# Query and key projections in thirds instead of halves, the keys' three pieces in one period, and the keys' split one period later

## The chip, the cores and the metric

One core of a Trainium2 chip runs the kernel. The metric is the device time of one launch in microseconds (us), lower is better. A core has five engines, each with its own program in its own order: PE (TensorE, matrix products), DVE (VectorE), ACT (ScalarE), POOL (GpSimd) and SP (SyncE, which only issues DMA transfers here). They wait for one another through semaphores.

## The reference

16 sequences of 512 tokens with 128 features go through one transformer layer in float32: attention with 16 heads of 8 features, then a mixture of 8 experts of which each token uses two, each followed by a residual sum and a layer norm.

```python
def attn(x, Wq, bq, Wk, bk, Wv, bv, Wo, bo):          # x: 16 x 512 x 128, 16 heads, dk = 8
    Q, K, V = heads(x @ Wq.T + bq), heads(x @ Wk.T + bk), heads(x @ Wv.T + bv)
    scores = jnp.einsum('bhqd,bhkd->bhqk', Q, K) / jnp.sqrt(jnp.float32(dk))
    probs = jax.nn.softmax(scores, axis=-1)
    intervened = probs.at[:, :, :, 0].set(0.0)
    intervened = intervened / jnp.clip(intervened.sum(axis=-1, keepdims=True), 1e-09, None)
    combined = probs + 0.5 * (intervened - probs)
    ...
    return attn_out @ Wo.T + bo
x = layernorm(x + attn(x, ...))
x = layernorm(x + moe(x, ...))       # 8 experts of 512, two for each token, silu(x w1) * (x w3) w2
```

## The kernel before

The kernel has an attention stage up to about 760 us, in which routing to the experts goes on beside it, an expert stage of 78 tiles of rows up to about 1131 us, and a final sum and layer norm.

**Units and periods.** A sequence's 16 heads are worked on in four groups of four; a group of a sequence is a unit, 64 in all. The attention stage is a pipeline of periods, one for each unit p = 4b + g (PERIODS, from -2 on). Here the periods g = 0, 1, 2, 3 of a sequence b are called its first, second, third and fourth. A period has eight steps k. In period p the unit p + 2 has its row maxima found (a bfloat16 product of queries and keys into the four banks of `mx_ps`, 128 queries at a time, in steps 0, 2, 4 and 6 on PE, L632, each followed by one DVE reduction over 128x2048 numbers, L1016); the unit p has its scores computed one bank at a time (L643) and turned into exponentials by ACT (L837); and the unit p - 1 has these multiplied with the values (L655), in the odd steps. The next `maxima` on PE waits for DVE's reduction, since there is one `mx_ps`.

**The ring.** Scores and all small products share three banks of PSUM, `ring_ps`, as a ring. Every product has a number (`ring_at`), which goes up in program order. PE may write number n when ACT is done with number n - 3; ACT empties them in the same order.

**The pieces behind.** The small products of other sequences are put behind the second score of a step, by the table `BEHIND`: (period in the sequence, step) gives a name and a distance in sequences. `q0`, `q1`, `k0` and `k1` are the projections of queries and keys, each of half of the 512 tokens (L673); q0, q1 and k0 of sequence b + 3 stand in the fourth period of b, and k1 of b + 2 in the first of b. `v0`, `v1` are the values of b + 1, `wo0`, `wo1` the output projection of b - 1, `px` a count for the routing. `BEFORE` lists those of sequence 0 ahead of the first period, `ONCE` those of the first periods -2 and -1. ACT adds the bias on the way out to `full` (L855). In the first period ACT also has `normed_rows` of b - 2 (L901) in every odd step.

**The split.** Queries and keys are split into three bfloat16 parts on POOL: `split_lead` (L1404: a cast, L1412, and a subtraction, L1414) and `split_rest` (L1416: L1421, L1423). SP stores the parts to memory (`store_parts`), from where they are loaded again by head for later units. For sequence 0 DVE does the split (`lead`, L988).

**Order on POOL.** It is written out by hand, for each of the four periods (L1585 to L1657). `beside_reduction(p, w)` makes POOL wait until PE has filled `mx_ps` for the w-th reduction of the period. In the first period the queries' lead stands beside reduction 0, their rest beside 2, and the keys' lead beside 3, followed by a scatter of routed rows. In the second period come `finish_sent` of b - 2 and a scatter beside reduction 0, `split_negmax` of the next unit (L1399, L1401), `product_of_sums` of b - 1 (L1454) and a scatter beside 1, `normalise_second` (L1459) beside 2. The keys' rest stands in the third period beside 2.

**Order on DVE.** Beside the reductions: in the second period `second_sums` (L1032) after reduction 0 and `reciprocals` (L1037) after reduction 1. The latter has its own wait, for POOL's product:

```python
            def reciprocals(b):
                dve.wait_ge(s_norm, NORM * b + 2)
                V.reciprocal(recips[:, 0, :], recips[:, 0, :]).then_inc(s_norm, 1)
```

## Time and profile before

| | us |
|---|---|
| three runs | 1175.75, 1178.43, 1179.16 |
| median | 1178.43 |
| the profiled execution, time | 1177.16 |
| the profiled execution, span from the first to the last instruction | 1175.0 |

Busy over the span: PE 1116.9 us (95%), DVE 927.2 (79%), ACT 824.8 (70%), POOL 663.2 (56%). The granted clock of TensorE is full (2.4 GHz) nearly all the time (0.997 on the mean).

In the profile, times are us from the start of the span unless marked ns; L673 is line 673 of the kernel. A row of the timeline has the start, the duration, the engine, the line, the operation, what it writes and reads, how often in a row (x4 is four instructions that are shown as one), and in brackets how long the engine was idle before and who ended that. Instructions of an engine overlap in part, so that one may start before the one ahead of it has ended. A float32 product appears as two records with half of the work each.

### The profile page before, as it was taken

The page shows a single profiled execution, that of the slowest core. Times are in us where ns is not written, and L with a number is a line of the kernel's source. Part 1 is how long each engine was busy: PE and PEld are TensorE (multiplying, and loading weights), DVE is VectorE, ACT ScalarE, POOL GpSimd, SP SyncE. Part 2 cuts the span into 40 slices and gives each one's busy share as a digit, 9 for nine tenths or more (in the row PEclk, how much of TensorE's full clock was granted, in tenths as well). Part 3 has the DMA queues.
Part 4 walks back from the last instruction along what each step waited for, and adds up shares of the span by engine and source line. Part 5 has one row for each costly group of instructions (what it writes and reads, how often), then busy time and mean ns, then how long its engine had stood idle before and what let it go on. Part 6 is the DMA issues. An engine that isn't in the chain of part 4 may idle for free. (4 is left out here: it accounts for less than half of the span.)

```text
span 1175.0 us, 23587 instructions
## 1 busy us (share of the span) xinstructions
PE 1116.9 (95%) x7236; PEld 575.7 (49%) x7240; DVE 927.2 (79%) x1421; ACT 824.8 (70%) x1668; POOL 663.2 (56%) x1003
## 2 busy tenths in 40 slices
PE   9999999999999999999999998999999999999986
PEld 6422232232222222222322222279999999999962
DVE  6888999999999999999999999855545554444435
ACT  2588888988889889888889888853544434345627
POOL 4424556666676676676676654666545433334336
PEclk9999999999999999999999999999999999999998
DMA  4453334444434343443443345353434333332247
GB/s 145 148 159 112 106 119 124 132 126 127 126 119 138 117 134 117 131 130 109 135 129 125 123 144 159 92 120 84 89 77 103 87 76 80 78 71 58 58 152 301
DMA packets 175051, 139.79 MB, mean 119 GB/s; under 512 B 89539, under 2 KB 151623, under 8 KB 174928
## 3 DMA queue, kind: packets, MB, share of 16 engines
q1 hardware_dynamic: 165672, 119.95, 36.3%
q0 software_dynamic: 8688, 18.14, 4.6%
q8 instruction: 60, 0.98, 0.4%
q14 instruction: 63, 0.52, 0.1%
q10 hardware_dynamic: 568, 0.20, 0.1%
HBM read 95.96 MB, written 42.19 MB: 118 GB/s over the span
## 5 line engine op out<-in xcount | busy, mean ns | idle before, releaser
L837 ACT ACTIVATE probs_sb<-ring_ps 128x512 f32<-128x512 f32 x1024 | 558.4, 598 | 96.9 <-PE ring_ps L643 81.1
L1016 DVE TENSOR_REDUCE rowmax_sb<-mx_ps 128x4 f32<-128x2048 f32 x256 | 586.0, 2289 | 26.3 <-PE mx_ps L632 20.7
L643 PE MATMUL ring_ps<-region_sb 74*128 74x512 bf16 x1024 | 311.4, 384 | 2.1 <-ACT probs_sb L837 2.0
L655 PE MATMUL acc_ps<-probs_sb,values_sb 128*32 128x512 f32 x2048 | 272.3, 604 | 0.0
L1690 POOL DMA_INDIRECT y_d<-probs_sb,values_sb x135 | 133.0, 985 | 190.0 <-DVE probs_sb L1329 166.0
L643 PEld LDWEIGHTS ring_ps<-region_sb 74*128 74x128 bf16 x1024 | 79.2, 97 | 312.8 <-ACT probs_sb L837 272.4
L912 ACT ACTIVATE xT_sb<-region_sb 128x512 f32 x78 | 49.2, 630 | 183.1 <-PE mx_ps L762 181.7
L1329 DVE SCALAR_TENSOR_TENSOR probs_sb<-ring_ps,values_sb 128x128 f32<-128x128 f32 x135 | 42.1, 347 | 143.2 <-issue 120.9
L1546 POOL DMA_INDIRECT rows_d<-sent_sb,pos_sb x128 | 130.1, 1016 | 41.2 <-issue 19.2
L632 PE MATMUL mx_ps<-k_maxima_sb,q_maxima_sb 32*128 32x512 bf16 x1024 | 101.0, 384 | 40.4 <-DVE rowmax_sb L1016 39.9
L783 PE MATMUL ring_ps<-region_sb,probs_sb 128*128 x1080 | 133.5, 275 | 1.6 <-DVE probs_sb L1339 1.6
L783 PEld LDWEIGHTS ring_ps<-region_sb,probs_sb 128*128 128x128 f32 x1080 | 131.0, 192 | 5.0 <-issue 2.2
L752 PE MATMUL mx_ps<-k_parts_sb,xT_sb 128*128 128x256 f32 (+1 forms) x624 | 130.5, 352 | 1.0 <-DVE k_parts_sb L1311 1.0
L1339 DVE TENSOR_TENSOR probs_sb<-mx_ps,probs_sb 128x512 f32<-128x512 f32 (+1 forms) x156 | 95.2, 619 | 25.9 <-PE mx_ps L762 18.6
L752 PEld LDWEIGHTS mx_ps<-k_parts_sb,xT_sb 128*128 128x128 f32 x624 | 106.8, 190 | 13.9 <-DVE k_parts_sb L1311 2.2
L655 PEld LDWEIGHTS acc_ps<-probs_sb,values_sb 128*32 128x32 f32 x2048 | 40.5, 108 | 97.9 <-issue 97.5
L632 PEld LDWEIGHTS mx_ps<-k_maxima_sb,q_maxima_sb 32*128 32x128 bf16 x1024 | 25.7, 90 | 111.7 <-DVE rowmax_sb L1016 102.8
L958 ACT ACTIVATE probs_sb<-mx_ps 128x1024 f32<-128x1024 f32 (+1 forms) x78 | 70.4, 903 | 4.5 <-PE mx_ps L752 4.4
L762 PE MATMUL mx_ps<-k_parts_sb,full_q_sb 128*128 128x256 f32 (+1 forms) x312 | 65.5, 353 | 0.0
L762 PE MATMUL mx_ps<-k_parts_sb,full_k_sb 128*128 128x256 f32 (+1 forms) x312 | 64.6, 350 | 0.0
L762 PEld LDWEIGHTS mx_ps<-k_parts_sb,full_q_sb 128*128 128x128 f32 x312 | 51.6, 191 | 5.3 <-issue 0.8
L1399 POOL CAST negmax_parts_sb<-negmax_sb 16x128 bf16<-16x128 f32 x64 | 17.9, 279 | 62.9 <-PE mx_ps L632 62.7
(193 smaller groups left out, 1174.6 us busy)
## 6 DMA issues: line engine op xcount, KB each, us to landing
region_sb<-q_parts_d SPq DMA_DIRECT2D x64, 288.0 KB
region_sb<-k_parts_d SPq DMA_DIRECT2D x64, 288.0 KB
k_parts_d<-k_parts_sb SPq DMA_DIRECT2D x46, 256.0 KB, 2.5
k_maxima_sb<-k_parts_d SPq DMA_DIRECT2D x128, 64.0 KB
probs_sb<-y_d SPq DMA_DIRECT2D x32, 256.0 KB, 6.9
q_maxima_sb<-q_parts_d SPq DMA_DIRECT2D x126, 64.0 KB
values_sb<-rows_d SPq DMA_DIRECT2D x57, 132.0 KB, 2.3
q_parts_d<-q_parts_sb SPq DMA_DIRECT2D x15, 384.0 KB
```

The lines of the kernel that those rows point to most:

```text
L632: last = nc.tensor.matmul(mx_ps[:, j, :], q[rows, P * c:P * (c + 1)], k[rows, :], start=True, stop=True)
L643: nc.tensor.matmul(bank, KS[b % 2][0:KR + MR, h, P * c:P * (c + 1)], QS[b % 2][0:KR + MR, h, :], start=True, stop=True).then_inc(s_ring_re ...
L655: last = nc.tensor.matmul(acc_ps[VW * j:VW * (j + 1), 0, :], VE[b % 2][:, c, HG * g + j, :], PT[u % 2][:, j, c, :], start=(c == 0), stop=( ...
L752: last = nc.tensor.matmul(up_ps[:, c, 0:n], W1T[t % 2][:, P * c:P * (c + 1)], XGT[t % 2][:, 0:n], start=True, stop=True)
L762: last = nc.tensor.matmul(lin_ps[:, c, 0:n], W3T[t % 2][:, P * c:P * (c + 1)], XGT[t % 2][:, 0:n], start=True, stop=True)
L783: last = nc.tensor.matmul(y_ps[:, at:at + D], HH[t % 2][:, c, P * w:P * (w + 1)], W2[:, bass.ds(expert + c * D, D)], start=(c == 0), stop= ...
L837: nc.scalar.activation(PT[u % 2][:, i // QC, i % QC, :], ring_bank("st", u, i), ACT.Exp, scale=SCALE).then_inc(s_ring_done, 1)
L958: nc.scalar.activation(SG[t % 2][:, :, 0:n], up_ps[:, :, 0:n], ACT.Silu).then_inc(s_silu, 1)
L1016: V.tensor_reduce(rowmax[u % 2][:, :].rearrange("p (j c) -> p j c", c=QC)[:, :, c], mx_ps[:, :, :], axis=AXX, op=ALU.max, negate=True).the ...
L1339: V.tensor_tensor(HH[t % 2][:, part, 0:n], lin_ps[:, part, 0:n], SG[t % 2][:, part, 0:n], ALU.mult)\
L1546: G.indirect_dma_start(rows_d, bass.IndirectOffsetOnAxis(ap=pos[b % 2][:, s, c:c + 1], axis=0), XE[b % 2][:, c, s, :], None).then_inc(s_sc ...
L1690: G.indirect_dma_start(y_d, bass.IndirectOffsetOnAxis(ap=XG[t % RING][:, w, D:D + 1].bitcast(i32), axis=0), YO[t % YRING][:, w, :], None, ...
```

## The change

- `half` becomes `third`: tokens 0 to 176, 176 to 344 and 344 to 512. Queries and keys are projected in three pieces each, q0, q1, q2, k0, k1, k2; a piece is written to its own columns of its bank.
- `BEHIND`: q0, q1, q2 of b + 3 in the fourth period, in the steps where q0, q1 and k0 stood. k0, k1, k2 of b + 2 in the first period, steps 3, 5 and 7, where only k1 stood, in step 3.
- `BEFORE` and `ONCE` have the new pieces; the keys of sequence 1 now stand in the first three steps of period -1.
- Who waited for q1 or k1 waits for q2 or k2.
- On POOL the keys' `split_lead` moves from the end of the first period (beside reduction 3) to the second period, right after the wait for its reduction 0, ahead of `finish_sent`.

```diff
-        BEHIND = {(0, 3): ("k1", 2), (1, 3): ("v0", 1), (1, 5): ("v1", 1), (1, 7): ("px", -2),
-                  (2, 5): ("wo0", -1), (2, 7): ("wo1", -1), (3, 3): ("q0", 3), (3, 5): ("q1", 3), (3, 7): ("k0", 3)}
-
-        BEFORE = (("q0", 0), ("q1", 0), ("k0", 0), ("k1", 0))
+        BEHIND = {(0, 3): ("k0", 2), (0, 5): ("k1", 2), (0, 7): ("k2", 2), (1, 3): ("v0", 1), (1, 5): ("v1", 1), (1, 7): ("px", -2),
+                  (2, 5): ("wo0", -1), (2, 7): ("wo1", -1), (3, 3): ("q0", 3), (3, 5): ("q1", 3), (3, 7): ("q2", 3)}
+
+        BEFORE = (("q0", 0), ("q1", 0), ("q2", 0), ("k0", 0), ("k1", 0), ("k2", 0))
         ONCE = {(-2, 1): ("gc", 0), (-2, 2): ("gw", 0), (-2, 3): ("v0", 0), (-2, 4): ("v1", 0), (-2, 5): ("q0", 1),
-                (-2, 6): ("q1", 1), (-2, 7): ("k0", 1), (-1, 0): ("k1", 1)}
+                (-2, 6): ("q1", 1), (-2, 7): ("q2", 1), (-1, 0): ("k0", 1), (-1, 1): ("k1", 1), (-1, 2): ("k2", 1)}
...
-        def half(name):
-            return slice(L // 2 * int(name[1]), L // 2 * (int(name[1]) + 1))
+        def third(name):
+            edges = (0, 176, 344, L)
+            return slice(edges[int(name[1])], edges[int(name[1]) + 1])
...
-                    last = nc.tensor.matmul(bank[:, 0:L // 2], (wq_sb if name[0] == "q" else wk_sb)[:, :],
-                                            xT_sb[b % 2][:, half(name)], start=True, stop=True)
+                    last = nc.tensor.matmul(bank[:, third(name)], (wq_sb if name[0] == "q" else wk_sb)[:, :],
+                                            xT_sb[b % 2][:, third(name)], start=True, stop=True)
...
-                    done = nc.scalar.activation(full[which][:, half(name)], bank[:, 0:L // 2], ACT.Identity,
+                    done = nc.scalar.activation(full[which][:, third(name)], bank[:, third(name)], ACT.Identity,
...
-                pool.wait_ge(s_ring_done, ring_at[("q1", "k1")[which], b] + 1)
+                pool.wait_ge(s_ring_done, ring_at[("q2", "k2")[which], b] + 1)
...
                     beside_reduction(p, 3)
-                    if is_seq(b + 2):
-                        split_lead(b + 2, 1)
                     scatter_chunk(b - 3, 1)
                 elif g == 1:
                     beside_reduction(p, 0)
+                    if is_seq(b + 2):
+                        split_lead(b + 2, 1)
                     if is_seq(b - 2):
                         finish_sent(b - 2)
                     scatter_chunk(b - 3, 2)
```

## Rows read from the trace of the kernel before

**Rows 1.** Windows, first period: length, busy PE, PEld, DVE, ACT, POOL, clock, DMA.
```profile
404.51:415.80 11.29, 10.34 (x68) 2.65 (x67) 11.09 (x15) 10.63 (x25) 7.88 (x10) 1.00 0.41 129
```

**Rows 2.** Timeline of DVE in the second period of b = 8.
```profile
415.80 2.29 DVE L1016 TENSOR_REDUCE rowmax_sb<-mx_ps 128x4 f32<-128x2048 f32 x1
418.01 0.27 DVE L1032 SCALAR_TENSOR_TENSOR recips_sb<-TN_sb 128x64 f32<-128x64 f32 x1
...
418.60 2.29 DVE L1016 TENSOR_REDUCE rowmax_sb<-mx_ps 128x4 f32<-128x2048 f32 x1 [0.23 <-PE mx_ps L632]
420.81 0.54 DVE L1037 RECIPROCAL recips_sb<-recips_sb 128x64 f32<-128x64 f32 x1
421.47 2.29 DVE L1016 TENSOR_REDUCE rowmax_sb<-mx_ps 128x4 f32<-128x2048 f32 x1
...
424.33 2.29 DVE L1016 TENSOR_REDUCE rowmax_sb<-mx_ps 128x4 f32<-128x2048 f32 x1
...
427.20 2.29 DVE L1016 TENSOR_REDUCE rowmax_sb<-mx_ps 128x4 f32<-128x2048 f32 x1
```

**Rows 3.** Timeline of PE: a half of the keys (k1), v0, and the maxima behind each.
```profile
409.16 0.60 PE L673 MATMUL ring_ps<-xT_sb,wk_sb 128*128 128x256 f32 x2
409.69 0.40 PE L632 MATMUL mx_ps<-k_maxima_sb,q_maxima_sb 32*128 32x512 bf16 x4
...
420.46 0.63 PE L690 MATMUL ring_ps<-wv_gate_sb,xT_sb 128*128 128x136 f32 x4
421.02 0.39 PE L632 MATMUL mx_ps<-k_maxima_sb,q_maxima_sb 32*128 32x512 bf16 x4
```

**Rows 4.** Timeline of DVE: the fourth period with the projections, and without (b = 13).
```profile
438.63 2.29 DVE L1016 TENSOR_REDUCE rowmax_sb<-mx_ps 128x4 f32<-128x2048 f32 x1
...
450.00 2.29 DVE L1016 TENSOR_REDUCE rowmax_sb<-mx_ps 128x4 f32<-128x2048 f32 x1
...
666.38 2.29 DVE L1016 TENSOR_REDUCE rowmax_sb<-mx_ps 128x4 f32<-128x2048 f32 x1
...
677.69 2.29 DVE L1016 TENSOR_REDUCE rowmax_sb<-mx_ps 128x4 f32<-128x2048 f32 x1
```

**Rows 5.** Timeline of ACT in the first period: k1 and normed_rows.
```profile
409.86 0.47 ACT L855 ACTIVATE full_k_sb<-ring_ps,bk_sb 128x256 f32<-128x256 f32 x1
410.21 0.49 ACT L901 ACTIVATE sent_sb<-ysum_sb,shift_sb,rstd_sb 128x128 f32<-128x128 f32 x1
...
415.49 0.48 ACT L901 ACTIVATE sent_sb<-ysum_sb,shift_sb,rstd_sb 128x128 f32<-128x128 f32 x1
```

**Rows 6.** Timeline of POOL from the keys' lead to the product of sums.
```profile
412.97 0.61 POOL L1412 CAST k_parts_sb<-full_k_sb 128x512 bf16<-128x512 f32 x1 [0.94 <-PE mx_ps L632]
413.66 1.16 POOL L1414 TENSOR_TENSOR full_k_sb<-full_k_sb,k_parts_sb 128x512 f32<-128x512 f32 x1
...
416.11 0.60 POOL L1521 COPY sent_sb<-sent_sb 128x512 f32<-128x512 f32 x1
...
417.65 1.06 POOL L1546 DMA_INDIRECT rows_d<-sent_sb,pos_sb  x1 [0.45 <-ACT probs_sb L837]
418.73 0.28 POOL L1399 CAST negmax_parts_sb<-negmax_sb 16x128 bf16<-16x128 f32 x1
...
419.48 0.34 POOL L1454 TENSOR_TENSOR recips_sb<-recips_sb,TN_sb 128x64 f32<-128x64 f32 x1
```

**Rows 7.** Timeline at the start: ACT's last piece of the queries, then POOL.
```profile
28.84 0.47 ACT L855 ACTIVATE full_q_sb<-ring_ps,bq_sb 128x256 f32<-128x256 f32 x1 [2.12 <-PE ring_ps L673]
...
29.38 0.61 POOL L1412 CAST q_parts_sb<-full_q_sb 128x512 bf16<-128x512 f32 x1 [0.60 <-ACT full_q_sb L855]
```

**Rows 8.** Timeline in the expert stage: a POOL addition and DVE's second_sums.
```profile
773.68 1.28 POOL L1479 TENSOR_TENSOR x_sb<-x_sb,bo_sb 128x512 f32<-128x512 f32 x1
773.77 1.32 DVE L1032 SCALAR_TENSOR_TENSOR recips_sb<-TN_sb 128x64 f32<-128x64 f32 x1
```

**Rows 9.** Timeline of SP: the move of the negated maxima.
```profile
419.54 1.20 SPq L482 DMA_DIRECT2D region_sb<-negmax_parts_sb  x2
```

More of the change, by code:

```diff
@@ L667, in behind @@
                 bank = ring_bank(name, b)
-                if name in ("q0", "q1", "k0", "k1"):
+                if name in ("q0", "q1", "q2", "k0", "k1", "k2"):
                     if name == "q0":
@@ L850, in behind @@
                 bank = ring_bank(name, b)
-                if name in ("q0", "q1", "k0", "k1"):
+                if name in ("q0", "q1", "q2", "k0", "k1", "k2"):
                     which = int(name[0] == "k")
@@ L990, in lead @@
                 exact, parts, n = full[which], qk_parts[which], 3 * which
-                dve.wait_ge(s_ring_done, ring_at[("q1", "k1")[which], 0] + 1)
+                dve.wait_ge(s_ring_done, ring_at[("q2", "k2")[which], 0] + 1)
                 V.tensor_copy(parts[:, 0, :], exact[:, :]).then_inc(s_first_split, 1)
```

## Prediction

> **What bounds the kernel now.** I read the stage table first, then the DVE, PE, ACT and POOL timelines of one sequence in the middle (b = 8, 404.51 to 450.00 us). In the first attention period of that sequence DVE is busy 11.09 of 11.29 us, PE 10.34, ACT 10.63, POOL 7.88 [rows 1]. The start times of the row-maximum reduction tell why. It takes 2.29 us, and the next one starts 2.80 us after it where nothing comes between (415.80 to 418.60) [rows 2]: there is one `mx_ps`, so PE can refill it only when the reduction has ended, and DVE waits about 0.5 us for that. Four of these make a period; 2.80 us is the floor, and whatever reaches past the 0.5 us gap, on PE before the next maxima or on DVE between two reductions, is paid in full. So there are two questions: what do the pieces do to PE's stretch before the maxima, and does anything that DVE waits for arrive later.
>
> **Part 1, the matmul pieces.** Two records for 256 columns hold PE from 409.16 to 409.69, where the maxima start, 0.53 us [rows 3]. That interval of reductions is 2.83 and not 2.80, so the cover is 0.50 us and a half is 0.03 us too long. Four records of 136 columns take 0.56 us (420.46 to 421.02) [rows 3], two would take 0.28. A third has two records of at most 176 columns. Between 0.28 for 136 and 0.53 for 256 it comes to 0.28 + 40/120 x 0.25 = 0.36 us: under the cover, free in all six places. What the halves cost now can be read off: the fourth period takes 11.37 us with q0, q1 and k0 (438.63 to 450.00) and 11.31 us where these are absent (666.38 to 677.69) [rows 4]; the first period takes 11.29 [rows 1] against 4 x 2.80 and 0.06 for the transpose at its end, 11.26. That is 0.09 us for a sequence. Each of the two sets of places occurs 14 times, so the gain is 14 x 0.09 = 1.3 us, and no more, since these are all the places where a half delays PE.
>
> **Part 2, the ACT evictions.** A half holds ACT 0.35 us before its next instruction (409.86 to 410.21) [rows 5]. A third costs between 0.24 (by its columns) and 0.35 us (all fixed); I take 0.30, the middle. The first period had one half and gets three thirds: 3 x 0.30 - 0.35 = 0.55 us more, 10.63 + 0.55 = 11.18 of 11.26 us [rows 1]. It fits, barely. The fourth period gets 3 x 0.30 in place of 3 x 0.35. I put this at nothing; its cover is ACT's idle 0.08 us in a period and the three banks of the ring. If all thirds cost 0.35, it is 11.33 against 11.26, 0.07 us for a sequence, 1.0 us in all.
>
> **Part 3, the keys' split one period later.** This is the edit that decides. On POOL the lead of the keys' split is a cast and a subtraction, 412.97 to 413.66 + 1.16 = 414.82, 1.85 us [rows 6]. It moves from the end of the first period to the head of the second, ahead of `finish_sent`, a scatter, the split of the negated maxima and `product_of_sums`. DVE takes `reciprocals` in program order after the second reduction of that period, and it waits for `product_of_sums`. Today the product starts at 419.48, takes 0.34 and is ready at 419.82; DVE comes to the reciprocals at 420.81 [rows 2, 6]. The cover is 0.99 us, and 1.85 us are put ahead of it. Queued behind the waiting reciprocals are the third reduction, behind it PE's next maxima, and so the whole period.
>
> When can the lead start? After the eviction of k2, which stands where `normed_rows` starts now, 415.49 [rows 5]; with 0.40 us to its end (0.30 to 0.47 by bounds: 0.47 is the half's duration) and 0.07 for the hand-over to POOL (28.84 + 0.47 to 29.38) [rows 7], at 415.96. It could not be earlier than the reduction of 415.80 [rows 2], since POOL waits for that. Then POOL is busy without a gap, with the steps that the rows have: 415.96 + 1.85 + 0.08 = 417.89 `finish_sent`; + 1.54 (416.11 to 417.65) = 419.43 scatter; + 1.08 (417.65 to 418.73) = 420.51 split of the negated maxima; + 0.75 (418.73 to 419.48) = 421.26 product; + 0.34 = 421.60 [rows 6]. With 0.05 for the hand-over DVE starts the reciprocals at 421.65 instead of 420.81. They take 0.54 [rows 2], so the third reduction starts at 422.19 instead of 421.47: 0.72 us late. The matmuls of v1 in the next interval lose their own 0.06 (2.86 instead of 2.80), since PE has waited meanwhile: 0.66 us net.
>
> One thing may add to it. At 773.77 the same `second_sums`, 0.27 us otherwise, took 1.32 us and ended 0.13 us after a POOL addition that had started 0.09 us before it [rows 2, 8]: the one engine held the other up. In the new order `finish_sent` starts with a copy of 0.60 us at 417.89, next to `second_sums` at 418.01. Whoever comes first, the other waits: DVE's wait (until about 418.6) has ended before the reciprocals and is covered; POOL's is between 0 and 0.2 us and is not. I take 0.07, so 0.73 us for a sequence.
> The Trainium skill's page "SBUF — State Buffer", section "Who interferes with whom", states this as a rule: a DVE instruction with two SBUF inputs contends with a GpSimd instruction that reads SBUF, and the second to issue blocks fully. By that rule the wait is sure if they overlap and the sum would have 0 or some 0.2 us, by who is first; without it, 0. The row agrees with the rule.
>
> How often? The lead exists for b up to 13, the product from b = 1, `finish_sent` from b = 2, the scatter from b = 3. Without the scatter (1.08 us) the product would come at 420.52, in time. So eleven sequences pay, b = 3 to 13: 11 x 0.73 = 8.0 us (bounds: 11 x 0.5 = 5.5 with a lead that starts with the reduction at 415.80 and nothing added, and 11 x 0.86 = 9.5 with 0.2 from the shared access).
>
> The rest of the queues. SP moves the negated maxima at 419.54 now [rows 9] and would do so at about 421.3; queued behind are the load of x, the store of the queries' parts and the loads for later units. The first score of the next period needs that move at 427.20 [rows 2], so 4 us of cover remain of 6. The keys' store stands in the fourth period behind the second half of the split, which stays in the third; the lead is done a whole period before. The scatters are moved with POOL and only the next-but-one sequence needs their buffer. All at nothing.
>
> **Start.** Two more evictions before the first maxima and pieces in the three first steps of period -1, where PE also has filler matmuls: 0 to 0.7 us (twice the 0.35 of a half) [rows 5]; I take 0.3. After attention nothing changes, and a delay there moves the whole rest.
>
> **Sum.** 8.0 - 1.3 + 0.3 = +7.0 us. The profiled execution took 1177.16 us (span 1175.0, 2.2 around it): 1184.2. The three runs have 1175.75, 1178.43 and 1179.16, mean 1177.8, median 1178.43; on the mean the sum gives 1184.8, and I predict that.
>
> **Rivals.**
> A, not slower: the product arrives in time. It decides at 420.81: the lead and the four steps would have to come to under 5.0 us from 415.80, where the rows have 1.85 + 0.08 + 1.54 + 1.08 + 1.09 = 5.64. For it: a step could shrink, such as the 0.45 us gap ahead of the scatter. Against it: 0.34 + 0.75 + 1.08 are real work, and the steps repeat in all sequences. Then only the gain is left: 1177.8 - 1.3 + 0.3 = 1176.8.
> B, slower still: ACT becomes the bound of the first period and POOL loses 0.2 us to the shared access. Evictions of 0.35 us and both holding 0.07 us, 14 times, with 11 x 0.86 and 0.7 at the start: 9.5 - 1.3 + 1.0 + 0.7 = +9.9, 1187.7. For it: ACT has only 0.08 us left. Against it: the ring takes up a short overrun, and today's half with a larger piece ran 2.83.
> C, the change does not do what it says: the split waits elsewhere or the delay is half as large, for instance when PE or DVE wins it back later in the period. Then +3.0, 1180.8. Against it: the floor of 2.80 leaves nowhere to win it back.
>
> **How the numbers follow.** Forecast 0.72, B 0.10, A 0.10, C 0.05, and 0.03 for a gain from something I don't see. A measurement of this kernel can tell about 0.3%, 3.5 us, from no change. Forecast and B are slower, 0.82; A and C the same, 0.15; faster 0.03. The range: the low end of the delay, 5.5 - 1.3 = +4.2, on the lowest run (1175.75) is 1180.0; the high end is B with some noise of the runs, 1190. It leaves out A, part of C and the unseen gain.
>
> **What would show it.** In the profile after: an idle time of DVE before the reciprocals, released by POOL's product, in eleven sequences, some 0.8 us each, and second periods of some 12.1 instead of 11.4 us [rows 2]; the matmuls of a third at 0.36 us and reductions at 2.80 around them; the fourth period at 11.31; ACT without waits from full evictions in the first period. Wrong would be a second period of 11.4 (A), or a first period longer than 11.3 (B).

## The result, and the profile after

The changed kernel takes 1180.18 us (median of 17 runs, 1179.08 to 1181.35), the kernel before, beside it on the same chip, 1176.58 us (17 runs, 1174.87 to 1179.16): ratio 1.0029, interval 1.0023 to 1.0035. It is 3.6 us slower; the forecast was +7.0 us and 1184.8. The direction and the place were right, the size was twice too large; 1180.18 is at the low end of the range of 1180.0 to 1190. The span of the profiled execution went from 1175.0 to 1179.0 us.

Head of the profile's page after, with busy time by engine, and from its table of waits the one on which the forecast rested (time in total, how often, the longest), for the stretch of attention:

```profile
span 1179.0 us, 23770 instructions
...
PE 1121.9 (95%) x7304; PEld 585.3 (50%) x7304; DVE 929.9 (79%) x1421; ACT 826.2 (70%) x1700; POOL 663.8 (56%) x1003
...
DVE recips_sb L1038 <- POOL recips_sb L1455: 7.8, 11, 0.7
```

Eleven waits of 0.7 us, where the kernel before has none of this kind. (All lines from about 330 on are one further down than before: L1037 is now L1038, L1454 is L1455.)

The second period of b = 8 again, the timeline of DVE and then of POOL after, to be read against [rows 2] and [rows 6]:

```profile
417.74 2.29 DVE L1017 TENSOR_REDUCE rowmax_sb<-mx_ps 128x4 f32<-128x2048 f32 x1
419.94 0.53 DVE L1033 SCALAR_TENSOR_TENSOR recips_sb<-TN_sb 128x64 f32<-128x64 f32 x1
...
423.54 0.55 DVE L1038 RECIPROCAL recips_sb<-recips_sb 128x64 f32<-128x64 f32 x1 [0.72 <-POOL recips_sb L1455]
424.01 2.23 DVE L1017 TENSOR_REDUCE rowmax_sb<-mx_ps 128x4 f32<-128x2048 f32 x1
426.16 0.40 DVE L1096 TENSOR_TENSOR H_sb<-absl_sb,rank_sb 128x32 f32<-128x32 f32 x1
...
426.84 2.28 DVE L1017 TENSOR_REDUCE rowmax_sb<-mx_ps 128x4 f32<-128x2048 f32 x1
...
429.69 2.29 DVE L1017 TENSOR_REDUCE rowmax_sb<-mx_ps 128x4 f32<-128x2048 f32 x1
```

```profile
417.94 0.61 POOL L1413 CAST k_parts_sb<-full_k_sb 128x512 bf16<-128x512 f32 x1 [1.81 <-PE mx_ps L633]
418.63 1.15 POOL L1415 TENSOR_TENSOR full_k_sb<-full_k_sb,k_parts_sb 128x512 f32<-128x512 f32 x1
419.74 0.60 POOL L1522 COPY sent_sb<-sent_sb 128x512 f32<-128x512 f32 x1
...
421.33 1.07 POOL L1547 DMA_INDIRECT rows_d<-sent_sb,pos_sb  x1 [0.44 <-issue]
422.41 0.28 POOL L1400 CAST negmax_parts_sb<-negmax_sb 16x128 bf16<-16x128 f32 x1
...
423.17 0.34 POOL L1455 TENSOR_TENSOR recips_sb<-recips_sb,TN_sb 128x64 f32<-128x64 f32 x1
...
425.44 1.07 POOL L1463 TENSOR_TENSOR T_sb<-TN_sb,recips_sb 128x512 f32<-128x512 f32 x1
```

POOL waits for no other engine from the keys' lead to the product (the 0.44 us ahead of the scatter are its own issue and stood there before), the reciprocals start when the product ends, and the third reduction starts 6.27 us after the first (before: 421.47 - 415.80 = 5.67). The period is 429.69 - 417.74 = 11.95 us long, before 11.39. The second half of the period has gained back 0.05: its two intervals are 2.83 and 2.85 us, before 2.86 and 2.87.

The row of 426.16 is a small collision of its own. This routing step of DVE takes 0.18 us in the kernel before; here it starts 0.72 us behind POOL's multiply into T2 and lasts until 426.56, when the multiply has ended (426.51). It is nearly hidden, since the reduction behind it follows at 2.83 us all the same. It comes back in the experiments.

The thirds and their copies (timelines of PE and ACT after, answering to [rows 3] and [rows 5]):

```profile
411.13 0.46 PE L674 MATMUL ring_ps<-xT_sb,wk_sb 128*128 128x176 f32 x2
411.63 0.39 PE L633 MATMUL mx_ps<-k_maxima_sb,q_maxima_sb 32*128 32x512 bf16 x4
...
411.83 0.40 ACT L856 ACTIVATE full_k_sb<-ring_ps,bk_sb 128x176 f32<-128x176 f32 x1
412.12 0.49 ACT L902 ACTIVATE sent_sb<-ysum_sb,shift_sb,rstd_sb 128x128 f32<-128x128 f32 x1
...
417.42 0.40 ACT L856 ACTIVATE full_k_sb<-ring_ps,bk_sb 128x168 f32<-128x168 f32 x1
```

Over the whole of attention, from the starts of the reductions: the second periods of b = 3 to 13 go from 11.39 to 11.95, each; the first from 11.29 to 11.26 and the fourth from 11.37 to 11.31; all others are as they were. At the start of the last unit the changed kernel is 4.84 us behind, at the first tile of the experts 5.44, at the end 4.0.

### The profile page after: what moved, and what is told of

Its sections match the earlier page's. It is cut to its first block, busy times and chain, and to the rows that moved or that the text cites. A ratio compares the mean times of both kernels' runs of the same rounds, so it can differ in the third digit from the quotient of the medians.

```text
span 1179.0 us, 23770 instructions
## 1 busy us (share of the span) xinstructions
PE 1121.9 (95%) x7304; PEld 585.3 (50%) x7304; DVE 929.9 (79%) x1421; ACT 826.2 (70%) x1700; POOL 663.8 (56%) x1003
## 4 chain that ended last, share of the span: by engine, by line
PE 50%; DVE 34%; issue 8%; POOL 5%; DMA 1%; SPq 1%; ACT 0%; ACTq 0%; POOLq 0%; DVEq 0%
DVE rowmax_sb L1017 27%; PE ring_ps L784 10%; PE mx_ps L753 10%; PE mx_ps L763 9%; PE ring_ps L644 6%; PE acc_ps L656 6%; PE mx_ps L633 4%; DVE TN_sb L1026 2%; PE mx_ps L815 1%; PE ring_ps L674 1%; POOL full_k_sb L1415 1%; POOL rows_d L1547 1%; DVE stats_sb L1049 1%; PE acc_ps L715 1%; PE ring_ps L815 1%
## 5 line engine op out<-in xcount | busy, mean ns | idle before, releaser
L763 PEld LDWEIGHTS mx_ps<-k_parts_sb,full_k_sb 128*128 128x128 f32 x312 | 51.1, 191 | 4.3
```

The source lines that it names most:

```text
L763: last = nc.tensor.matmul(lin_ps[:, c, 0:n], W3T[t % 2][:, P * c:P * (c + 1)], XGT[t % 2][:, 0:n], start=True, stop=True)
```

## The experiments

Every kernel was timed beside the kernel before on the same chip; ratios are to it. "Second period" is that of b = 3 to 13, read as the distance of reductions.

**The move alone, without the thirds** (e2), an edit of the kernel before:

```
                     beside_reduction(p, 3)
-                    if is_seq(b + 2):
-                        split_lead(b + 2, 1)
                     scatter_chunk(b - 3, 1)
                 elif g == 1:
                     beside_reduction(p, 0)
+                    if is_seq(b + 2):
+                        split_lead(b + 2, 1)
```

> The kernel before, in halves, with the keys' lead moved to the head of the second period as in the changed kernel, and nothing else. Theory: the delay comes with the move alone. With halves k1 is there long before, so the lead starts with the reduction, 0.16 us earlier than in the changed kernel, and the delay is 0.56 - 0.16 = 0.40 us for a sequence, 4.4 us in all, without the gain of the thirds: ratio 1.0037. Rival (the pieces): the same time as before.

Measured 1180.16 us, ratio 1.0027 (1.0017 to 1.0037). Second periods 11.72 us, +0.33 each, 3.57 us at the last unit. Waits of DVE in attention:

```profile
DVE recips_sb L1037 <- POOL recips_sb L1454: 5.3, 11, 0.5
```

The move makes the wait by itself. The second periods were expected 0.40 longer and are 0.33. With halves the keys are whole earlier, so the lead starts 0.03 us before the period's first reduction (417.37 and 417.40) instead of 0.20 behind it, and the delay is 0.23 smaller.

**A dose more** (e4), the changed kernel with the keys cast twice:

```
                 G.tensor_copy(parts[:, 0, :], exact[:, :]).then_inc(s_split_step, 1)
                 pool.wait_ge(s_split_step, 3 * n + 1)
+                if which == 1 and b >= 2:
+                    G.tensor_copy(parts[:, 0, :], exact[:, :]).then_inc(s_again, 1)
+                    pool.wait_ge(s_again, b - 1)
```

> The changed kernel with one more cast of the keys (0.61 us, and about 0.08 until the next step starts) in the keys' lead of every second period but the first ones: a dose more of what stands ahead of product_of_sums. Theory (POOL's chain to product_of_sums sets when DVE's reciprocals start): the wait of the reciprocals grows by 0.69 in each of 11 sequences, second periods 12.64 instead of 11.95, 7.6 us more than the changed kernel: 1187.8, ratio 1.0095 to the kernel before. If the later POOL multiplies meet DVE's two-input steps, up to 0.5 a sequence more: 1193. Rival (the chain is not what sets it): no longer than the changed kernel, 1180.2, 1.003.

Measured 1187.74 us, ratio 1.0090 (1.0075 to 1.0106); second periods 12.62.

```profile
DVE recips_sb L1039 <- POOL recips_sb L1459: 14.6, 11, 1.3
```

0.67 us for a cast of 0.61 and its hand-over: what is put on POOL ahead of the product costs its full length. This is shown by e2 and e4 together.

**The thirds without the move** (e6): the lead back at the end of the first period, ahead of the scatter there.

```
                     beside_reduction(p, 3)
+                    if is_seq(b + 2):
+                        split_lead(b + 2, 1)
                     scatter_chunk(b - 3, 1)
                 elif g == 1:
                     beside_reduction(p, 0)
-                    if is_seq(b + 2):
-                        split_lead(b + 2, 1)
```

> The changed kernel with the keys' lead back in the period in which it stood before, at the end of the first period, beside its fourth reduction and ahead of a scatter: the thirds alone, without the move by a period. The lead waits for the last third of the keys, whose copy in the changed kernel ended 0.1 us after the period's end (ACT at 417.42 for 0.40, the period's end at 417.74), and the scatter (1.2 with its start) that stood before the end of that period comes behind it, so that POOL's chain is later by 1.2 than in the changed kernel. My theory: product_of_sums later by 1.2, second periods 13.1 instead of 11.95, 12 to 13 us over the changed kernel, 1193 (1.014). Rival, that the place of the lead by period matters and the thirds themselves are free: the time of the kernel before, 1176.6 (1.000).

Measured 1203.61 us, ratio 1.0214 (1.0186 to 1.0243).

```profile
DVE recips_sb L1038 <- POOL recips_sb L1455: 21.1, 11, 1.9
```

Most second periods are 13.16, 1.21 more than in the changed kernel, as expected: the lead waits for the last third wherever it stands, and now a scatter stands behind it. So the move belongs to the thirds. The time was expected at 1193, though: the eleven delays make 11 x 1.21 = 13.3 of the 25.2 us by which the last unit is later than in the changed kernel. The rest lies in four sequences, b = 3, 6, 10 and 13, where second periods take 14.6 to 14.8 and third ones up to 15.0. Windows of that kernel (length, busy PE, PEld, DVE, ACT, POOL, granted clock, DMA share, GB/s), b = 3:

```profile
193.20:195.55 2.35, 2.35 (x18) 0.65 (x17) 0.47 (x2) 2.19 (x6) 2.09 (x5) 1.00 0.09 29
195.55:198.36 2.81, 1.20 (x10) 0.66 (x10) 2.78 (x5) 1.02 (x4) 2.41 (x5) 1.00 0.37 86
198.36:200.00 1.64, 1.64 (x11) 0.30 (x9) 1.64 (x2) 1.41 (x3) 1.49 (x2) 0.61 1.11 339
203.00:206.00 3.00, 3.00 (x12) 0.39 (x11) 2.76 (x4) 1.57 (x3) 2.12 (x2) 0.50 0.31 112
```

In the third interval of the second period PE is busy 1.20 of 2.81 us, since it has run ahead and its maxima wait for the late reduction; then the granted clock falls from 1.00 (2.4 GHz) to 0.50 (1.2 GHz) for some 13 us, less in the other three, and now PE holds up DVE. In b = 8 PE was as idle (1.19 of 2.82) and the clock stayed. So a delay of DVE can cost a second time on PE; which sequences it hits is open.

**The lead behind the product** (e1), an attempt to take the wait away:

```
                     beside_reduction(p, 0)
-                    if is_seq(b + 2):
-                        split_lead(b + 2, 1)
                     if is_seq(b - 2):
                         finish_sent(b - 2)
...
                         product_of_sums(b - 1)
+                    if is_seq(b + 2):
+                        split_lead(b + 2, 1)
                     scatter_chunk(b - 3, 3)
```

> The changed kernel with one edit on POOL: the keys' lead of the split stands in the second period behind product_of_sums instead of ahead of finish_sent. Theory (POOL's in-order chain makes the product late, DVE waits for it with the reciprocals): the waits of the reciprocals for the product are gone except the one in the tail, the eleven second periods of 11.95 us go back to 11.39, and the gain of the thirds stays, so 6.2 us less than the changed kernel and 1.3 us less than the kernel before, a ratio of 0.999 to before. Rival (the pieces themselves cost it, on ACT or in the ring): the time stays about 3.6 us above before, since no piece is moved.

Measured 1181.03 us, ratio 1.0034 (1.0021 to 1.0047). A miss: the wait for the product is gone from the table, and the second periods are 12.05 us, longer still. Timelines of DVE and POOL in e1, b = 8:

```profile
426.51 0.25 DVE L1096 TENSOR_TENSOR H_sb<-absl_sb,rank_sb 128x32 f32<-128x32 f32 x1
426.80 0.99 DVE L1102 TENSOR_TENSOR Hs_sb<-H_sb 128x32 f32<-128x32 f32 x1
427.71 0.21 DVE L1105 TENSOR_TENSOR factor_sb<-magnitudes_sb,top_sb 128x64 f32<-128x64 f32 x1
...
426.67 1.07 POOL L1463 TENSOR_TENSOR T_sb<-TN_sb,recips_sb 128x512 f32<-128x512 f32 x1
```

The second of DVE's routing steps (L1102) takes 0.19 us in the changed kernel; here it took 0.99 and ended with POOL's multiply into T2. In the changed kernel most of this multiply runs beside a reduction (425.44 to 426.51, reduction 424.01 to 426.24), which reads PSUM, and only its last 0.35 us meet a step (the row of 426.16 above). The multiply starts 1.43 us behind the third reduction there and 2.37 here: POOL's later work had moved it wholly under DVE's short steps between the third and fourth reduction.

**The same with halves** (e5): the kernel before with the lead behind the product, by the same edit.

> The kernel before, in halves, with the keys' lead behind product_of_sums in the second period. A control for the gain of the thirds: the place of the lead should cost nothing here, so the time is that of before (ratio 1.000), and the kernel with thirds and the same place of the lead should be 1.3 us faster than this one. If the lead in this place costs or gives something itself, both will differ from that by the same amount.

Measured 1205.0 us, ratio 1.0241 (1.0213 to 1.0270). The largest miss. Timelines and windows of e5:

```profile
435.17 0.99 DVE L1095 TENSOR_TENSOR H_sb<-absl_sb,rank_sb 128x32 f32<-128x32 f32 x1
436.19 0.19 DVE L1101 TENSOR_TENSOR Hs_sb<-H_sb 128x32 f32<-128x32 f32 x1
436.30 1.12 DVE L1104 TENSOR_TENSOR factor_sb<-magnitudes_sb,top_sb 128x64 f32<-128x64 f32 x1
...
435.05 1.07 POOL L1462 TENSOR_TENSOR T_sb<-TN_sb,recips_sb 128x512 f32<-128x512 f32 x1
436.26 1.08 POOL L1466 TENSOR_TENSOR T_sb<-TN_sb,recips_sb 128x512 f32<-128x512 f32 x1
...
437.35:440.34 2.99, 1.51 (x14) 0.85 (x11) 2.90 (x4) 1.06 (x3) 1.02 (x2) 0.91 0.43 155
440.34:444.23 3.89, 3.89 (x18) 0.66 (x16) 2.87 (x5) 2.03 (x4) 2.23 (x2) 0.63 0.22 73
```

POOL comes 0.28 us earlier within the period than in e1 (its copy waits for ACT's `normed_rows`, which have one third less ahead of them), and that is enough for two collisions instead of one. Twice DVE's step starts 0.12 or 0.04 us behind POOL's multiply and lasts until that ends. Second periods of 12.9 to 13.1 us follow, 17.3 us more in all. PE is idle for 1.48 us, and the granted clock falls from 1.00 to 0.50 (0.91 and 0.63 are the means of the two stretches). Eight of the eleven third periods take 12.4 to 15.0 us, 11.2 us more in all, so over a third of the loss is the clock's.

**One scatter behind the product** (e3), the changed kernel with `scatter_chunk(b - 3, 2)` moved:

```
-                    scatter_chunk(b - 3, 2)
                     beside_reduction(p, 1)
                     if is_unit(p + 1):
                         split_negmax(p + 1)
                     if is_seq(b - 1):
                         product_of_sums(b - 1)
+                    scatter_chunk(b - 3, 2)
```

> The changed kernel with the keys' lead where it is and scatter 2 of the second period behind product_of_sums. Theory: it is the length of the chain ahead of the product that counts and not what stands in it. Without 1.08 us of scatter and the 0.44 us gap ahead of it the product is ready 4.3 us after the first reduction, where DVE comes for it at 5.0: no wait, second periods of 11.39, 1.3 us less than before (ratio 0.999). Rival (the lead itself disturbs DVE or the ring in that place): the time stays near that of the changed kernel, 3.6 us above before.

Measured 1199.87 us, ratio 1.0177 (1.0145 to 1.0209). Again no wait for the product and again a miss: second periods 12.61, two steps of DVE at 0.72 and 1.11 us (338.33 and 339.19) beside POOL's multiplies (337.93 for 1.07, 339.14 for 1.08), and a granted clock of 0.53 on the mean of 344 to 348 us; four third periods take 13.66 instead of 11.43.

After three misses the theory had two terms: a late product, and a POOL multiply under DVE's two-input steps. It asks for an order of POOL in which the product is early and the multiply into T2 lies wholly inside a reduction.

**The lead in two pieces** (e7): its cast at the head of the second period, its subtraction right behind the product, and one scatter moved behind `normalise_second`.

```
                         product_of_sums(b - 1)
-                    scatter_chunk(b - 3, 3)
+                    if is_seq(b + 2):
+                        subtract_lead(b + 2, 1)
                     beside_reduction(p, 2)
                     if is_seq(b - 1):
                         normalise_second(b - 1)
+                    scatter_chunk(b - 3, 3)
```

> The changed kernel, with the keys' lead taken apart on POOL in the second period: its cast (0.61 us) stays at the head, its subtraction (1.15) stands right behind product_of_sums, and the third scatter of that stretch stands behind normalise_second instead of ahead of it. Reckoned from the changed kernel's rows with the period's first reduction at 0: cast to +0.8, the three steps of finish_sent to +2.1, scatter to +3.4, the maxima's split and product_of_sums to +4.6, before the third reduction can start (+5.1 after the second); subtraction to +5.8; the multiply into T2 at about +6.7 to +7.8, and DVE's two-input steps after the third reduction at +7.9. My theory (both a late product and a POOL multiply under DVE's two-input steps cost time) expects no wait of the reciprocals in the stretch of attention, second periods of 11.4 us, and a time 1.3 us under that of the kernel before: 1175.3, ratio 0.999. If only the amount of POOL's work in that period counted, it would stay at the changed kernel's 1180.2 (1.003).

**The whole lead behind the product, and the scatter moved** (e8), e1 with one line more:

```
-                    scatter_chunk(b - 3, 3)
                     beside_reduction(p, 2)
                     if is_seq(b - 1):
                         normalise_second(b - 1)
+                    scatter_chunk(b - 3, 3)
```

> The keys' lead behind product_of_sums, as in e1, and besides one scatter moved from ahead of normalise_second to behind it; POOL does the same work in the same period. In e1 the multiply into T2 ran from +8.0 to +9.1 after the period's first reduction, under DVE's two-input steps; here it should run from +6.9 to +7.9 and end about when they start. Theory (the collision of POOL's multiply with those steps made e1 slow): second periods 11.4 to 11.5 us instead of 12.05, the time 1175.3 to 1176.5, ratio 0.999 to 1.000. Rival (POOL's work of 1.8 us more in that period is the cause, wherever it stands): second periods stay at 12.0, 1181, ratio 1.003.

e7 measured 1174.33 us, ratio 0.9982 (0.9973 to 0.9991); e8 1174.24 us, ratio 0.9976 (0.9966 to 0.9986). Both have second periods of 11.39, and both beat the two kernels of this study: the thirds' gain without their price. Timelines of e8, b = 8:

```profile
419.18 0.35 POOL L1455 TENSOR_TENSOR recips_sb<-recips_sb,TN_sb 128x64 f32<-128x64 f32 x1
...
421.98 1.08 POOL L1463 TENSOR_TENSOR T_sb<-TN_sb,recips_sb 128x512 f32<-128x512 f32 x1
...
420.21 0.54 DVE L1038 RECIPROCAL recips_sb<-recips_sb 128x64 f32<-128x64 f32 x1
420.87 2.30 DVE L1017 TENSOR_REDUCE rowmax_sb<-mx_ps 128x4 f32<-128x2048 f32 x1
423.08 0.18 DVE L1096 TENSOR_TENSOR H_sb<-absl_sb,rank_sb 128x32 f32<-128x32 f32 x1
...
423.40 0.22 DVE L1105 TENSOR_TENSOR factor_sb<-magnitudes_sb,top_sb 128x64 f32<-128x64 f32 x1
```

The multiply ends at 423.06, the step starts at 423.08 and takes 0.18. POOL does the same work in the same period as in e1, so its amount is not what counts.

**Both moves with halves** (e10): the kernel before with the edits of e8.

> The kernel before (halves) with the two moves of e8: the keys' lead behind product_of_sums in the second period and one scatter behind normalise_second. Beside e8 it leaves out only the thirds; beside e5 it has only the scatter moved. In e5 the multiply into T2 ran from +7.75 to +8.82 after the period's first reduction and two of DVE's routing steps took 0.99 and 1.12 us under it and the next one; here it should run from +6.7 to +7.8 and end before them. Theory: no blocked step, no fall of the granted clock, second periods 11.39, fourth periods 11.37 as in the kernel before (the thirds' 1.3 us not gained): 1176.5, ratio 1.000. Rival (halves with the keys' lead in the second period are slow for another reason): third periods over 12 us again and 1190 or more. Second rival (e8's gain comes from the moves, not from the thirds): 1174.3, ratio 0.998.

Measured 1177.63 us, ratio 1.0008 (0.9999 to 1.0017). Second periods 11.39, no fall of the clock, fourth periods 11.36. Beside e5 this is one scatter moved, and 27 us. Beside e8 it shows what the thirds give: from the first reduction to the last unit e8 gains 1.34 us and e10 0.15.

**POOL writes instead of reading** (e9): e1, with the multiply into T2 replaced, so that this kernel leaves out the second term of the attention.

```
-                G.tensor_tensor(by_head(T2), SUMS[:, :, DK:2 * DK], per_head(2), ALU.mult).then_inc(s_norm, 1)
+                G.memset(T2[:, :, :, :], 0.0).then_inc(s_norm, 1)
```

> e1 (the keys' lead behind product_of_sums) with POOL's multiply into T2 replaced by a memset of T2 to zero, so the second term of the attention is left out: POOL then only writes SBUF in the place where it read two operands. Theory (DVE's two-input steps wait while POOL reads SBUF beside them): the steps L1096, L1102 and L1105 take 0.2 us each as in the kernel before, second periods 11.4 to 11.5 instead of e1's 12.05, time 1175.3 to 1176.5, ratio 0.999 to 1.000, unless the multiply into T1, which moves ahead with it, takes over the place (then 12.0 and 1181). Rival (what makes e1 slow is not on POOL's side of these steps): 12.05 and 1181, ratio 1.003, with the steps as long as in e1.

Measured 1174.82 us, ratio 0.9984 (0.9975 to 0.9993), second periods 11.39. Timelines of e9:

```profile
423.29 0.53 POOL L1463 MEMSET T_sb<- 128x512 f32 x1
...
423.11 0.28 DVE L1096 TENSOR_TENSOR H_sb<-absl_sb,rank_sb 128x32 f32<-128x32 f32 x1
423.43 0.19 DVE L1102 TENSOR_TENSOR Hs_sb<-H_sb 128x32 f32<-128x32 f32 x1
423.54 0.22 DVE L1105 TENSOR_TENSOR factor_sb<-magnitudes_sb,top_sb 128x64 f32<-128x64 f32 x1
```

The memset (423.29 to 423.82) lies over DVE's second and third step, and they take 0.19 and 0.22. Had it blocked, the step of 423.43 would have lasted to 423.82, 0.39 us. So a busy POOL alone does not block. The memset lacks the multiply's reads and its arithmetic; that it is the reads is borne out by POOL's copy of 419.74 in the changed kernel, which has no arithmetic and held `second_sums` up (0.53 instead of 0.27).

**The end of the kernel** (e11 to e14). After the first of the experts' tiles the changed kernel wins back 1.4 us that the sum did not have: the tiles take 2.1 us less, what follows them 0.6 more. From the first to the last down-projection of the experts' tiles the kernels with thirds take 350.8 to 352.1 us, those with halves (before, e2, e5, e10) 352.9 to 354.6, and the latter have a gap at 334.6 us after the first. Before, last tiles: SP's issues, a DMA queue that carries instructions (packets, MB, share of 1110 to 1112 us), and DVE:

```profile
1110.33 3.29 SPq L558 DMA_DIRECT2D values_sb<-rows_d  x4
...
q8 instruction: 1, 0.02, 4.6%
...
1115.52 0.31 DVE L1311 STREAM_TRANSPOSE k_parts_sb<-values_sb 128x128 f32<-128x128 f32 x1 [2.86 <-DMA values_sb<-rows_d]
```

Four issues take 3.29 us instead of 1.82 where a packet of instructions falls, and a tile waits 2.86 us for its rows. Sixteen waits more on SP and 36 more on ACT were the first guess:

```
             for p in PERIODS[1:]:
                 b, g = divmod(p, NG)
+                if 2 <= p < 18:
+                    sp.wait_ge(*split_done(0, 0))
```

> The kernel before with 16 waits more on SP, one in each of 16 periods of attention, on a semaphore that has long had its value: nothing waits for them. What they are to tell: from the first to the last of the experts' tiles the four profiles with halves took 352.9 to 354.6 us and the eight with thirds 350.8 to 352.1, with the same work, the same rows on SP and the same start, whatever the attention before them took. In all of them single DMA issues on SP take 0.8 to 1.7 us longer than the 0.45 of the others, about every 10 to 14 us, and at other tiles with thirds than with halves. If these long issues sit at fixed places of SP's stream of instructions, 16 instructions more move them by about a tile against the tiles, and the wait of 4.35 us at 334.6 us after the first tile (2.68 without it) moves or goes; the time changes by up to 2 us either way: 1174.6 to 1178. If they hang on the landing of transfers or on what the tiles wait for, all stays: the gap at 334.6, 353.9 us, 1176.8.

```
             for p in PERIODS:
                 b, g = divmod(p, NG)
+                if 2 <= p < 38:
+                    act.wait_ge(*split_done(0, 0))
```

> The kernel before with 36 waits more on ACT, one in each of 36 periods, on a semaphore that has long had its value: as many instructions more as the thirds bring on ACT, with no work. If the length of another engine's stream of instructions is what moves SP's long issues between halves and thirds, the tiles take 350.8 to 352.1 us from first to last as with thirds, without the wait at 334.6, and the time is 1.5 to 2 us under that of the kernel before: 1175.0 (0.9985). If only SP's own stream or something else of the thirds does it: 353.9 and 1176.8 (1.000). In attention no period longer by more than 0.05.

e11 measured 1176.97 us, ratio 1.0005 (0.9996 to 1.0013), e12 1177.39 us, ratio 1.0005 (0.9995 to 1.0014). The packet of 1111.3 us (before) starts at 1111.5 and 1111.6. The profile of e11 does not have the gap (351.0 us for the tiles), though the packet is there: it does not always cost. e12 has it, smaller (3.31, 352.6 us). In both, SP's four issues for that tile are over before the packet starts (1109.39 for 1.81 in e11, 1110.09 for 1.82 in e12), and it meets a later issue; why they are earlier is open.

Then TensorE's stream, with halves (e13) and with e8 (e14):

```
                 for k in range(STEPS):
+                    if 0 <= p < 62 and k % 4 == 3:
+                        pe.wait_ge(s_pool_const, 1)
                     c = k // 2
```

> The kernel before (halves) with 124 waits more on TensorE's stream, two in each of 62 periods of attention, on a semaphore that has long had its value: instructions without work, about as many as the thirds add there (64 matmul and 64 weight load records more). What it is to tell: in the traces of before and of the changed kernel the packets of 16 KB of the queue that carries instructions (60 in the kernel before) fall together with SP's long DMA issues: before at 1076, 1086, 1100, 1110 and 1122 us, that is 299, 309, 323, 334 and 346 us after the first tile's down-projection; in the changed kernel at 304, 316, 329 and 340. Theory (it is TensorE's stream that these packets bring, thirds shift where they fall among the tiles, and one that falls at 334 costs a tile's load its time): the packets move 5 to 6 us earlier against the tiles, the gap of 4.35 us at 334.6 goes, first to last tile 350.8 to 352.1 us instead of 353.9, time 1.5 to 2 us under that of the kernel before, plus what the waits cost in attention (0 if they are hidden). Rival (something else of the thirds): the packets and the gap stay, 353.9 us.

> e8 (thirds, 1174.2) with the same 124 waits more on TensorE's stream: by the theory the packets of instructions move another 5 to 6 us earlier against the tiles, together about one of their intervals (11.9 us on the mean) from where the kernel before has them, so the gap at 334.6 us after the first tile comes back, first to last tile takes about 353.9 us instead of 351.7, and the time is about 2 us over e8's: 1176.2, ratio 0.9995. Rival (what shortens the tiles is the thirds themselves): 351.7 us and 1174.2, ratio 0.998.

e13 measured 1175.92 us, ratio 0.9994 (0.9985 to 1.0004); e14 1175.46 us, ratio 0.9991 (0.9982 to 1.0000). In e13 the packets start at 1081.5, 1095.1, 1105.9 and 1120.0 us, where e8 has them at 1081.0, 1095.3, 1105.3 and 1116.1; the gap is gone, tiles 351.3 us. In e14 they start at 1076.0, 1086.7, 1100.2 and 1110.9, where the kernel before has 1076.3, 1087.1, 1100.5 and 1111.3, and the gap is back (3.8 us at 334.8; the tiles take 352.3, not the 353.9 expected):

```profile
1110.13 2.86 SPq L559 DMA_DIRECT2D values_sb<-rows_d  x4
...
1114.43 0.31 DVE L1314 STREAM_TRANSPOSE k_parts_sb<-values_sb 128x128 f32<-128x128 f32 x1 [1.83 <-DMA values_sb<-rows_d]
```

So the packets follow the number of TensorE's instructions, and are most likely these instructions; the thirds moved them. What it is worth is less sure. Against the kernel before, e13 gains 0.5 us of the 1.5 to 2 expected, within its interval of nothing. In its profile the tiles take 2.6 us less, and 0.5 of it is lost ahead of them by a blocked step of DVE in the last second period, which the next section comes to; e14 is 1.2 us over e8, by the ratios 1.8 us with some 1.6 either way. The place of the packets is shown; that it is worth all of the 1.4 us is not.

## Why the prediction was right or wrong, step by step

Two steps failed. The term of part 3, 11 x 0.73 = 8.0 us for the late product, was mis-sized: it measured 6.2. And "after attention nothing changes", put at nothing, was -0.8 us in the profiles. The mechanism, the place and the number of sequences held.

- **What bounds.** Right: 2.80 us from reduction to reduction, and a reduction that starts late is paid in full (e2, e4).
- **Part 1.** Right: 11.26 and 11.31 us for the first and fourth period. The first is 0.03 shorter in 13 sequences, the fourth 0.06 in 11 and 0.11 in two, 1.3 us in all; e10 against e8 gives 1.2. The price of 0.36 us for a third can't be read, as the maxima behind it wait for DVE (0.50 from 411.13 to 411.63).
- **Part 2.** Right: a third holds ACT for 0.29 us (411.83 to 412.12), 0.30 was taken; the first period did not get longer, so rival B falls.
- **Part 3, mechanism.** Right in each link. From the first reduction the product ends at +5.77 (423.51 - 417.74), 5.80 was reckoned. Eleven sequences and no others. Rivals A and C fall: the wait is there, and no more than 0.05 of it is won back within the period. C's number, 1180.8, is near the measured one, but by another way than C's.
- **Part 3, size.** The term was mis-sized: 11 x 0.73 = 8.0 us was 11 x 0.56 = 6.2. Three pieces of it: the hand-over and POOL's steps came to 0.05 less; the reduction follows the start of the reciprocals by 0.47 us, not 0.54 (423.54 to 424.01), 0.07; and the 0.07 for the shared access were not paid. Against these 0.19, the two intervals behind gave back 0.02 less than the 0.06 reckoned for v1, partly because of the step of 0.40. The second piece could have been read ahead: in [rows 2] DVE's next instruction starts 0.08 us before the reduction's 2.29 us are over (415.80 + 2.29 against 418.01). The collision was there: `second_sums` took 0.53 instead of 0.27 beside POOL's copy of 419.74. But DVE was the one that waited, under its cover, and POOL's copy took its 0.60.
The Trainium skill's page "SBUF — State Buffer", section "Who interferes with whom", has it that the second of the two to issue blocks fully; that is what the row of `second_sums` shows, and e5's rows of 0.99 and 1.12 us far better. At a distance of 0.02 us the recorded starts do not tell who was second (next rows).
- **Start.** 0.3 us was put in; the first reduction comes 0.32 later, period -2 is 0.36 shorter and period -1 0.05 longer, so nothing is left of it at period 0. In the other profiles the first reduction starts anywhere between 17.44 and 18.43 us, so this difference may be chance.
- **After attention "nothing changes".** Wrong by -0.8 us, in two places. In the last second period, b = 15, a two-input step of DVE lasted as long as POOL's multiply into T2, which is 0.6 us at the first tile. Timelines after, and behind them those before:

```profile
747.41 1.14 DVE L1105 TENSOR_TENSOR factor_sb<-magnitudes_sb,top_sb 128x64 f32<-128x64 f32 x1
...
747.39 1.07 POOL L1463 TENSOR_TENSOR T_sb<-TN_sb,recips_sb 128x512 f32<-128x512 f32 x1
...
742.56 0.21 DVE L1104 TENSOR_TENSOR factor_sb<-magnitudes_sb,top_sb 128x64 f32<-128x64 f32 x1
...
742.54 1.15 POOL L1462 TENSOR_TENSOR T_sb<-TN_sb,recips_sb 128x512 f32<-128x512 f32 x1
```

POOL's order in this period is the same in both kernels, and so is the multiply's place: 8.20 us after the period's first reduction, before 8.19. The step's start is recorded 0.02 us behind the multiply's both times; before, it was the multiply that got longer (1.15 instead of 1.07). Nor does it go by the thirds: the step is blocked in the profiles of e6 (thirds) and e13 (halves), the multiply in e1 and e4 (thirds) and in e2, e11 and e12 (halves). So these 0.6 us are not shown to come from the change; what decides is open. In the last tiles 1.4 us came back, with TensorE's instruction packets at other places.

The sum as measured: 6.2 - 1.3 + 0 + 0.6 - 1.4 = +4.1 us against +7.0, and 4.0 in the spans. Without the 0.6 it is 3.5, and the medians differ by 3.6; with one profile of each kernel that can be chance. Of the difference of 2.9, 1.8 is the mis-sized term, 0.3 the start, 0.8 what lies behind attention. The forecast also stood on a higher base: 1177.8, the mean of three runs, where 17 runs give 1176.58.

## What to carry to other kernels

When work is put on an in-order helper engine, follow every later step of that engine within the period, not only the one that is waited for: a step that was hidden beside a PSUM reduction can slide under the other engine's short SBUF steps, and then it costs more than the wait (e1, e3, e5). The work need not be given up for it: here one scatter moved past `normalise_second` turned 1205.0 into 1177.6 us with halves, and 1181.0 into 1174.2 with thirds. And two profiles that differ in the number of instructions differ in where instruction packets fall, so an end that moves by a microsecond need not have to do with the work that was changed. So it is, too, with two instructions that start 0.02 us apart on two engines that block each other: read such a place in several profiles before it goes into a sum.

## What was not expected of the hardware

- A DVE step with two SBUF inputs that starts 0.04 to 0.72 us behind a POOL multiply which reads SBUF lasts until that multiply ends: 0.99 instead of 0.19 us in e1, 1.12 instead of 0.22 in e5, 0.40 instead of 0.18 in the changed kernel. At 0.02 us it went both ways with the same instructions: 1.14 us in the changed kernel, e6 and e13; 0.21, with the multiply at 1.15, in the kernel before, e1, e2, e4, e11 and e12. Beside a memset of 0.53 us the step takes 0.19 (e9), and a reduction from PSUM beside the multiply its usual 2.3 us.
- After an interval in which PE was busy 1.20 of 2.81 us the granted clock fell from 1.00 to 0.50 for some 13 us (e6, b = 3), and not after an interval like it (b = 8). This turned a delay of 1.2 us in a sequence into some 4 us in the four sequences that it hit.
- A packet of 16 KB of instructions (most likely TensorE's) that falls beside SP's DMA issues goes with 3.29 us for four issues instead of 1.82, and 124 more waits on TensorE moved these packets by 6 us against the tiles. It does not always cost: in e11 the four issues were over before the packet, and the gap is gone.
